# Attention over two layers: the second layer's score maxima taken for several heads by one VectorE instruction

## What is computed

```python
# 32 query heads of 16, 8 key/value heads; each key head serves 4 query heads
scores = einsum('bqhd,bkhd->bhqk', xq, xk) / sqrt(16)
scores = where(tril(ones(s, s)), scores, -inf)        # causal; s = 1024
probs = softmax(scores, axis=-1)
out = einsum('bhqk,bkhd->bqhd', probs, xv) @ Wo
```

## Time and profile before

| what | us |
|---|---|
| median of 3 runs | 2045.32 |
| lowest, highest | 2042.33, 2059.11 |
| the profiled execution | 2046.85 |
| its span in the trace | 2045.3 |

### The profile page before, as it was taken

The page is one execution under the profiler, slowest core; times in us unless marked ns, Lnnn a source line. Parts: engine busy times, 40 slices in busy tenths (PEclk is TensorE's granted clock), DMA queues, the critical chain, the costliest instruction groups (busy, mean ns, idle before and its releaser), DMA issues.

```text
span 2045.3 us, 29252 instructions
## 1 busy us (share of the span) xinstructions
PE 1932.7 (94%) x10864; PEld 973.7 (48%) x10864; DVE 1405.1 (69%) x1879; ACT 1094.6 (54%) x2177; POOL 233.4 (11%) x606
## 2 busy tenths in 40 slices
PE   6999999998999999999999999997899999999998
PEld 5888887633333333333333357443433333333436
DVE  6554545328999999999988736369677777777643
ACT  3221211232887887878777743024176666767562
POOL 1000000000000100001000000000124334232230
PEclk9999999996999999999999999998699999999799
DMA  6010100141222112211121001014212121221102
GB/s 207 1 47 1 43 1 1 33 143 41 45 42 61 32 32 42 44 30 31 32 56 30 8 21 38 0 31 120 62 29 47 31 51 29 48 46 31 28 10 86
DMA packets 79212, 87.53 MB, mean 43 GB/s; under 512 B 19072, under 2 KB 52864, under 8 KB 79072
## 3 DMA queue, kind: packets, MB, share of 16 engines
q1 hardware_dynamic: 79072, 85.67, 16.8%
HBM read 55.20 MB, written 20.71 MB: 37 GB/s over the span
## 4 chain that ended last, share of the span: by engine, by line
PE 79%; DVE 9%; ACT 7%; issue 2%; SPq 1%; DMA 1%; POOL 0%; DVEq 0%; POOLq 0%
PE ps L1373 19%; PE ps L1403 11%; PE ps L1088 7%; PE ps L1089 7%; PE ps L1090 7%; ACT arena L738 6%; PE ps L1399 6%; PE ps L1320 6%; PE ps L1228 4%; PE ps L1326 4%; DVE arena L996 4%; PE ps L1182 3%; PE ps L1323 1%; PE ps L1258 1%; SPq L430 1%
## 5 line engine op out<-in xcount | busy, mean ns | idle before, releaser
L996 DVE TENSOR_REDUCE arena<-ps 128x1 f32<-128x1024 f32 (+7 forms) x1024 | 976.6, 987 | 204.6 <-PE ps L1323 123.7
L738 ACT ACTIVATE arena<-ps 128x512 f32<-128x512 f32 (+3 forms) x1792 | 869.1, 555 | 396.9 <-PE ps L1399 203.0
L1373 PE MATMUL ps<-arena 128*17 128x512 f32 (+3 forms) x3584 | 436.8, 560 | 0.4 <-POOL arena L561 0.4
L1326 PE MATMUL ps<-slots 48*128 48x512 f32 x1024 | 409.8, 477 | 9.8 <-DVE arena L996 8.5
L1403 PE MATMUL ps<-slots 50*128 50x512 f32 x1024 | 383.7, 454 | 22.8 <-ACT arena L738 13.9
L1403 PEld LDWEIGHTS ps<-slots 50*128 50x128 f32 x1024 | 170.8, 186 | 319.2 <-ACT arena L738 273.3
L1320 PE MATMUL ps<-slots 96*128 96x512 bf16 (+3 forms) x768 | 221.1, 345 | 24.9 <-DVE arena L996 13.1
L1399 PE MATMUL ps<-slots 98*128 98x512 bf16 (+3 forms) x768 | 218.3, 335 | 6.2 <-ACT arena L738 3.3
L1326 PEld LDWEIGHTS ps<-slots 48*128 48x128 f32 x1024 | 172.0, 191 | 58.5 <-DVE arena L996 33.5
L561 POOL TENSOR_SCALAR_AFFINE_SELECT arena<-arena 128x128 f32<-128x128 f32 x512 | 146.4, 293 | 382.9 <-ACT arena L738 371.8
L622 ACT ACTIVATE xn<-ps 128x512 f32<-128x512 f32 (+1 forms) x44 | 26.3, 598 | 259.6 <-PE ps L1090 259.6
(11 more groups left out here) (126 smaller groups left out, 1796.1 us busy)
## 6 DMA issues: line engine op xcount, KB each, us to landing
slots<-qparts SPq DMA_DIRECT2D x96, 128.0 KB, 3.6
qparts<-arena SPq DMA_DIRECT2D x32, 256.0 KB
xnT<-arena SPq DMA_DIRECT2D x256, 32.0 KB
slots<-qparts SPq DMA_DIRECT2D x96, 64.0 KB, 3.3
qparts<-arena SPq DMA_DIRECT2D x48, 128.0 KB
slots<-qparts SPq DMA_DIRECT2D x32, 192.0 KB, 3.7
w_raw<-in_wgu SPq DMA_DIRECT2D x20, 256.0 KB, 3.2
acc<-in_x SPq DMA_DIRECT2D x4, 1024.0 KB, 7.5
```

Source lines behind the costliest of these rows:

```text
L738: act.activation(prob[local % P_RING][:, q0:CH], bank(local % SP_RING)[:, q0:CH], ACT.Exp, scale=SCALE).then_inc(S["p_ready"], 1)
L996: dve.tensor_reduce(maxes[c][:, h * TPC + qt:h * TPC + qt + 1], src[:, 0:max_width(l == 1, c, qt)], AX_X, ALU.max).then_inc(S["x_done"], 1)
L1326: last = pe.matmul(dst[:, k0:k1], q_slot[u][r:r + ROWS[0], c, h % 2, qt * P:(qt + 1) * P].bitcast(F32R), k_slot[u][r:r + ROWS[0], k0:k1].b ...
L1373: mm = pe.matmul(bank(7)[32 * h:32 * h + DH + 1, q0:CH], v_slot[n % SLOTS][:, kt, :], prob[idx % P_RING][:, q0:CH], start=(kt == 0), stop= ...
```

## The change

In the second layer a piece may now hold several heads. `segment` gives the columns that one head takes in the bank pair of 1024 (128, 256, 512 or 1024), and `head_sets` puts together as many heads as fit: four at 128 and 256 keys, two at 384 and 512, one above that. Half 0 of a block so has 1 + 1 + 2 + 2 = 6 pieces instead of 16, half 1 still 16. Where heads are together they come in the order 0, 1, 2, 3; else as before. TensorE makes the same matmuls, each head's into its own columns; only the first waits (`opens`) and only the last raises `x_ready` (`closes`). VectorE's reduce reads a three-dimensional operand (queries, heads, keys) and writes one maximum per head. `pace` gives a piece the cost of its last head's keys + 100 + the columns ahead of that head. The `NORMS` steps are put between pieces with a spacing `step` that follows the number of pieces (3 in the first layer as before, 1 in the second). In the first layer all else stays the same too.

```diff
-def max_blocks():
-
-    heads = (2, 0, 3, 1)
+def head_sets(causal, c, qt):
+
+    together = min(HG, 2 * CH // segment(causal, c, qt))
+    if together == 1:
+        return [(h,) for h in (2, 0, 3, 1)]
+    return [tuple(range(h, h + together)) for h in range(0, HG, together)]
+
+
+def max_blocks(causal):
+
     blocks = []
     for n in range(B * NG):
-        r = [[(n, c, qt, h) for qt in range(TPC) for h in heads] for c in range(QC)]
+        r = [[(n, c, qt, heads) for qt in range(TPC) for heads in head_sets(causal, c, qt)] for c in range(QC)]
...
+            step = (len(r[0]) - 2) // len(NORMS)
             for i, norm in enumerate(NORMS):
-                first = first + r[0][2 + 3 * i:5 + 3 * i] + [norm]
-            first = first + r[0][2 + 3 * len(NORMS):]
+                first = first + r[0][2 + step * i:2 + step * (i + 1)] + [norm]
+            first = first + r[0][2 + step * len(NORMS):]
...
+def segment(causal, c, qt):
+
+    w = max_width(causal, c, qt)
+    return P if w == P else 2 * P if w == 2 * P else CH if w <= CH else 2 * CH
...
                     if qt is not None:
-                        dve.tensor_reduce(maxes[c][:, h * TPC + qt:h * TPC + qt + 1], src[:, 0:max_width(l == 1, c, qt)],
+                        w, seg = max_width(l == 1, c, qt), segment(l == 1, c, qt)
+                        if len(h) == 1:
+                            dve.tensor_reduce(maxes[c][:, h[0] * TPC + qt:h[0] * TPC + qt + 1], src[:, 0:w],
+                                              AX_X, ALU.max).then_inc(S["x_done"], 1)
+                            return
+                        dve.tensor_reduce(maxes[c].rearrange("p (h t) -> p h t", t=TPC)[:, h[0]:h[-1] + 1, qt],
+                                          src[:, 0:len(h) * seg].rearrange("p (h s) -> p h s", s=seg)[:, :, 0:w],
                                           AX_X, ALU.max).then_inc(S["x_done"], 1)
...
-                def max_piece(j, n, c, qt, h, k0, k1, w):
-
-                    dst = bank(3 + 2 * (j % 2), 2)
+                def max_piece(j, n, c, qt, h, k0, k1, w, of, opens, closes):
+
+                    dst = bank(3 + 2 * (j % 2), 2)[:, of:]
...
-                    if k0 == 0 and j >= 2:
+                    if opens and j >= 2:
...
-                    if k1 == w:
+                    if closes:
                         last.then_inc(S["x_ready"], 1)
...
+                        w, seg = max_width(causal, item[1], item[2]), segment(causal, item[1], item[2])
+                        for i, h in enumerate(item[3]):
+                            for k0 in range(0, w, CH):
+                                k1 = min(w, k0 + CH)
+                                r.append((starts[n] + e,) + item[:3] + (h, k0, k1, w, i * seg, i == 0 and k0 == 0,
+                                                                        i == len(item[3]) - 1 and k1 == w))
...
-                    cost = [900 if item[1] is None else 0 if item[3] is None else w + 100 for *item, k0, k1, w in todo]
...
+                    for j, n, c, qt, h, k0, k1, w, of, opens, closes in todo:
+                        cost = 900 if n is None else 0 if qt is None else w + 100 + of
+                        at.append(before + (0 if causal else cost * k0 // w))
+                        before += cost if closes else 0
```

More of the change, by code:

```diff
@@ L103, in max_width, with norms_through @@
     return (TPC * qc + qt + 1) * P if causal else N
-def norms_through():
-    items = [item for block in max_blocks() for item in block]
+def segment(causal, c, qt):
+    w = max_width(causal, c, qt)
+    return P if w == P else 2 * P if w == 2 * P else CH if w <= CH else 2 * CH
+def norms_through(causal):
+    items = [item for block in max_blocks(causal) for item in block]
     return items.index(NORMS[-1]) + 1
@@ L715, in xo_high @@
                     if c < QC:
-                        act.wait_ge(S["x_done"], norms_through())
+                        act.wait_ge(S["x_done"], norms_through(l == 1))
                     else:
@@ L1017, in _ @@
                 done = 0
-                for n, block_ in enumerate(max_blocks()):
+                for n, block_ in enumerate(max_blocks(l == 1)):
                     if n == GROUPS - 4:
@@ L1298, in _ @@
                 before_end = 6 * KC + 1
-                blocks = max_blocks()
+                blocks = max_blocks(l == 1)
                 items_in_all = sum(len(b) for b in blocks)
                 starts = [sum(len(b) for b in blocks[:n]) for n in range(GROUPS)]
-                def max_piece(j, n, c, qt, h, k0, k1, w):
-                    dst = bank(3 + 2 * (j % 2), 2)
+                def max_piece(j, n, c, qt, h, k0, k1, w, of, opens, closes):
+                    dst = bank(3 + 2 * (j % 2), 2)[:, of:]
                     if n is None:
@@ L1334, in pieces @@
                     for e, item in enumerate(blocks[n]):
-                        if lo <= e < hi:
-                            w = 1 if item[2] is None else max_width(causal, item[1], item[2])
-                            r += [(starts[n] + e,) + item + (k0, min(w, k0 + CH), w) for k0 in range(0, w, CH)]
+                        if not lo <= e < hi:
+                            continue
+                        if item[2] is None:
+                            r.append((starts[n] + e,) + item + (0, 1, 1, 0, True, True))
+                            continue
+                        w, seg = max_width(causal, item[1], item[2]), segment(causal, item[1], item[2])
[4 more added lines that the diff above has]
+                                                                        i == len(item[3]) - 1 and k1 == w))
                     return r
@@ L1344, in pace @@
                 def pace(todo):
-                    cost = [900 if item[1] is None else 0 if item[3] is None else w + 100 for *item, k0, k1, w in todo]
                     at, before = [], 0
-                    for (*item, k0, k1, w), c in zip(todo, cost):
-                        at.append(before + (0 if causal else c * k0 // w))
-                        before += c if k1 == w else 0
+                    for j, n, c, qt, h, k0, k1, w, of, opens, closes in todo:
+                        cost = 900 if n is None else 0 if qt is None else w + 100 + of
+                        at.append(before + (0 if causal else cost * k0 // w))
+                        before += cost if closes else 0
                     return [OFFSET[l] + a * MAX_END[l] * group_items / max(1, before) for a in at]
@@ L1355, in first_piece @@
                     j, n = piece[:2]
-                    if n is not None and j == starts[n] and piece[5] == 0:
+                    if n is not None and j == starts[n] and piece[-2]:
                         pe.wait_ge(S["slot_in"][n % SLOTS], (n // SLOTS + 1) * (16 * 12))
```

## The result

The changed kernel takes 2012.57 us in the median of four runs (2005.0 to 2019.69), the kernel before 2044.13 in the same job (four runs, 2042.33 to 2059.11). The ratio is 0.9837 with a 95% interval of 0.98 to 0.9873: faster by 1.6%, where 2021 had been forecast. The profiled execution took 2015.05 us, span 2013.5, mean granted clock 0.975.

The account below looks back on a forecast made before the run. TensorE, busy 94% of the span, was taken as the bound, so VectorE savings pay only where TensorE waits. Gains of 18.6 + 2.5 + 3 + 1.5 = 25.6 us off 2046.85 gave 2021.3, forecast as 2021 us, range 2009 to 2039.

Parts of the forecast that it names:

- Both ends must move, or nothing does: End of a group's first half: TensorE's own work and the copy-store-rows DMA chain end nearly together, 0.58 us apart.
- The first four products: Start of a group: 4th product at +1.80 us, 0.89 us earlier, with short matmuls at 0.06 us each.
- The second half: Second half of a group: one 640-key piece moves ahead and a 0.37 us wait goes, gaining 0.7 us.
- a steady group: Second layer's attention: 0.9 us from the first half plus 0.7 from the second, 1.6, taken as 1.55.
- The 12 groups: Groups 1 to 10, 12 and 14: 1.55 us gained in each, 18.6 us in all.
- The prologue with group 0: Start of the second layer's attention: 1.8 us gained in the prologue, 2.5 with the slower part of group 0.
- Group 11: Wait behind the reciprocal and a half-clock stretch: between 0 and 5 us gained, taken as 3.
- Group 13: Group with the four norm steps: half-clock stretch remains, 1.5 us gained, between -3 and 5 for a shifted clock edge.
- The first item of my list: VectorE's reduces in the first halves: 16 become 6, saving 1.56 us a group, 25 us over sixteen.
- The chain did not absorb it: Rival at the half boundary: fourth exponential not earlier, only 12.5 us gained, 2034 us; chance 0.32 for 2028 to 2040.
- The merged reduce: Rival on VectorE: 157 ns per head or more, 0.3 to 0.5 us a group less, 2026; within the forecast's 0.6.
- The falling clock: Rival at each boundary's DMA wait: half clock in 14 groups costs 28 to 48 us, 2049 to 2069; chance 0.08.

Follow-up runs that it names:

- early_transpose_after: Changed kernel with the transpose of the last group's maxima after a block's first set instead of its second; 2034.2 us, ratio 0.9943 to the kernel before.
- rows_first_early: Changed kernel with the maxima rows sent ahead of the output's store and the transpose after a block's first set; 2010.15 us, ratio 0.9814 to the kernel before.
- rows_first_after: Changed kernel with the maxima rows sent ahead of the output's store; 2006.6 us over four runs, 2009.29 us over six when timed longer.
- rows_first_before: Kernel before with the second layer's maxima rows sent ahead of the store of the previous group's output; 2036.36 us, ratio 0.9963 to the kernel before.
- after_again: Changed kernel, nothing altered, run again for a second trace; 2011.22 us.
- pairs_only: Changed kernel with at most two heads a set and the transpose third, within the first four products; 2026.06 us, ratio 0.9906 to the kernel before.

## Why the prediction was right, and where its sum was short

**The bound.** "Both ends must move, or nothing does" held. I had read it from group 4, one of four groups in that trace (2, 4, 8 and 12) whose second half waits for the DMA; in most, as in group 5 here, TensorE goes straight on, at +11.50:

```profile
1643.41 0.39 PE L1399 MATMUL ps<-slots 98*128 98x512 bf16 x1
```

Moving the copy and moving the rows in the kernel before are both tests of the DMA's end alone: first halves of 11.44 and 11.48 us. TensorE's end is moved all but alone in `early_transpose_after`, where SP's first store comes only 0.19 us earlier than before (+4.08 against +4.27) and TensorE, ready earlier, waits 1.0 us for the rows: 11.31, just these 0.19 less. With both moved it is 10.57 (the change), and with the DMA's end out of the way 10.22 (`rows_first_early`) and 10.15 (`rows_first_after`). That the DMA chain is late last after the change is shown by removing it: intervals of 29.64 instead of 30.21 in the mean.

**The first four products.** Each step came out within 0.05 us. The spacing of short matmuls was 0.06 us (four heads of 128 from 1565.58 to 1566.05, 0.47 for the eight), so keeping the row was right. The 81 ns that the Trainium skill (TensorE: Matmul & The Clock Gate, Back-to-back issue gap) gives for a load and a matmul of 128 columns does not hold for this pattern: here it is 59 ns.

**The second half.** 20.24 became 19.48, 0.76 against 0.7: 0.51 less of TensorE's busy time and 0.25 less of its idle time. The wait of 0.37 us did not go wholly, as I wrote; one of 0.19, behind the transpose's `sem_inc`, took its place. With 0.93 in the first half (11.50 to 10.57) a steady group gave 1.7 rather than 1.55; I had rounded 1.6 down. The 12 groups: 17.2 + 1.7 + 1.4 = 20.2 us against 18.6.

**The prologue with group 0**: 3.5 against 2.5. The prologue itself, from the first maxima to the first product of group 0, went from 25.70 to 22.79 us, so 2.9, the top of my range for it, where I took 1.8. Part of it is clock: the half-clock stretch there is 30.7 us long before and 23.9 after.

**Group 11**: 4.3 against 3. The reciprocal is covered as forecast down to a wait of 0.85 us before the set of 384, and the clock did not fall in either trace of the changed kernel; in the kernel before it fell in both. In `rows_first_before` it did not fall, behind the same wait, and the interval is 33.08: some 2.2 of the 4.3 us are clock, and 2.1 the rest.

**Group 13 is the term that was mis-sized**: 1.5 forecast, 10.2 in the two first traces. The second trace of before splits it: 45.61 - 38.63 = 7.0 us belonged to a half-clock stretch of one execution, and 38.63 - 35.45 = 3.2 us to the change. Not that the edge shifted, as I wrote, but that it wasn't there. With 3.2 for it, the gains are 20.2 + 3.5 + 4.3 + 3.2 = 31.2 us. A term that I left out goes against them: the 1.4 us behind the last mark are there in the second pair of traces too, and both traces of the changed kernel have 3.4 us at half clock there, from 1989.4 and 1985.7, which neither trace of before has. That leaves 29.8, where 25.6 was forecast; the second pair of traces is 29.5 us apart, the medians 31.6. The forecast was short because the steady groups were rounded down and the prologue and groups 11 and 13 were sized too low. How near it came is partly luck: the second layer's start moved by 5.8 us between the two traces of the changed kernel.

**What I argued from the wrong end.** The first item of my list, 25 us of VectorE's time, is real (25.5 us less busy) and earns next to nothing here.

**The rivals.** The chain did not absorb it: the copy came 0.9 us earlier. The merged reduce was not dearer. The falling clock was not the rule in the changed kernel. It did come behind late rows once in `after_again`, and in `early_transpose_after`, where the chain ends later, only three of ten intervals are undisturbed. But the length of one wait does not decide it: in group 11 it fell behind 1.51 us in the kernel before and not behind 1.52 in `rows_first_before`, and in `pairs_only` it fell behind one boundary wait of 2.21 us and not behind one of 2.24. What does decide stays open. The kernels with the rows first have no boundary wait for the DMA and not one disturbed interval among the steady ones.

## What to carry to other kernels

When two engines hand buffers back and forth, look at what releases the next phase before you count an engine's busy time: here more than half of a group's gain came from clearing four handoffs from ahead of the one product that starts a 7 us chain through ScalarE and SP, and shortening TensorE's own way to the same point with it. If two chains end a phase together, shorten both or expect next to nothing, and test it by moving each alone. A DMA that a phase waits for should be issued ahead of stores in the same list that nobody waits for yet.

## What the runs showed of the hardware

In the traces of the two kernels, of `pairs_only` and of `early_transpose_after`, TensorE went on 1.14 to 1.17 us after the issue of the two small DMAs of the maxima rows had ended wherever it waited for them (1.25 once), but 3.2 us after it in one group of `after_again` (1567.43 to 1570.63) and some 2.7 in two groups of `pairs_only` and one of `early_transpose_after`; I found nothing in the program to tell these groups apart. Stretches at 1.2 GHz come and go between executions of one program: 20.5 us in group 13 in one trace of before and none in the other; and from 1071 us on, in the first layer, 3.4 us in the first trace of before, none there in that of the changed kernel and 37.5 us in that of the kernel with pairs. Comparing intervals inside the traces settled differences of 0.08 us a group that the times of whole runs, spread over 15 us and more, could not.
